# A six-layer block on one core: the two expert phases written out, with turns two tiles behind, the router in two parts and the output stored in quarters

## What is computed

```python
logits = xf @ gate_w                      # gate_w is 128 x 8
scores = softmax(logits)
top_scores, top_idx = top_k(scores, 2)
scale = zeros((T, 8)).at[arange(T)[:, None], top_idx].set(top_scores)
xs = scale.T[:, :, None] * xf[None, :, :]
h = silu(einsum('etd,edh->eth', xs, w1)) * einsum('etd,edh->eth', xs, w3)
out = einsum('eth,ehd->etd', h, w2).sum(axis=0)   # 8 experts, hidden 64
```

## Time and profile before

| | |
|---|---|
| runs, us | 2304.22, 2305.01, 2311.65 (median 2305.01) |
| profiled execution, its own time | 2300.82 us |
| its span, first to last instruction | 2299.0 us |
| mean granted TensorE clock | 0.959 of full speed |
| busy PE / DVE / ACT / POOL | 2071.4 / 1740.1 / 1378.8 / 1001.9 us |
| DMA | 144.78 MB, mean 63 GB/s |

### The profile page before, as it was taken

One profiled execution on the slowest core, in us unless ns is written; L12 is line 12 of the kernel. 1 busy time (PEld: TensorE's weight loads), 2 busy tenths in 40 slices (PEclk: granted clock), 3 DMA queues, 4 the chain that ended last, 5 costly groups with the idle time before them and its releaser, 6 DMA issues. The chain is left out here.

```text
span 2299.0 us, 41230 instructions
## 1 busy us (share of the span) xinstructions
PE 2071.4 (90%) x14740; PEld 1520.2 (66%) x14740; DVE 1740.1 (76%) x3007; ACT 1378.8 (60%) x2687; POOL 1001.9 (44%) x1475
## 2 busy tenths in 40 slices
PE   5899999987999987999999868799999999998978
PEld 4576666755777764767667645577686776775745
DVE  5766666666777758666666755599999999999953
ACT  1666666664777764666666643548558477575422
POOL 2445454524666655454555403043343443333423
PEclk7899999998999997999999989899999999999979
DMA  5555555520000005555555431000000000000000
GB/s 167 140 141 139 136 141 140 142 53 1 2 1 2 1 3 132 138 139 141 142 137 138 112 145 44 0 1 1 1 1 1 1 1 1 1 1 0 1 14 19
DMA packets 147459, 144.78 MB, mean 63 GB/s; under 512 B 14272, under 2 KB 107072, under 8 KB 146368
## 3 DMA queue, kind: packets, MB, share of 16 engines
q1 hardware_dynamic: 127680, 132.78, 21.2%
q10 hardware_dynamic: 19584, 9.44, 2.3%
HBM read 93.94 MB, written 38.80 MB: 58 GB/s over the span
## 5 line engine op out<-in xcount | busy, mean ns | idle before, releaser
L614 DVE TENSOR_REDUCE sb_f_mx<-ps_f_s 128x2 f32<-128x512 f32 x768 | 504.3, 686 | 250.3 <-PE ps_f_s L352 248.7
L538 ACT ACTIVATE sb_f_pt<-ps_f_t 128x1024 f32<-128x1024 f32 x384 | 382.0, 1024 | 62.7 <-PE ps_f_t L369 56.5
L1968 POOL TENSOR_TENSOR sb_mb_h<-sb_mb_h 128x512 f32<-128x512 f32 x128 | 165.9, 1317 | 490.7 <-DVE sb_mb_h L1828 490.7
L352 PE MATMUL ps_f_s<-sb_f_stack 96*128 96x256 bf16 x1536 | 287.9, 280 | 25.9 <-DVE sb_f_mx L614 12.8
L1823 DVE TENSOR_TENSOR_SCAN sb_mb_h<-sb_mb_da,sb_mb_h 128x1024 f32<-128x1024 f32 x128 | 291.1, 2313 | 2.1 <-ACT sb_mb_da L1687 2.1
L1536 PE MATMUL ps_mb_f<-sb_mb_fc,sb_mb_cw 128*128 128x256 f32 x1280 | 285.3, 381 | 2.0 <-ACT sb_mb_fc L1701 2.0
L1536 PEld LDWEIGHTS ps_mb_f<-sb_mb_fc,sb_mb_cw 128*128 128x128 f32 x1280 | 240.4, 190 | 37.0 <-ACT sb_mb_fc L1701 4.3
L1687 ACT ACTIVATE sb_mb_da<-sb_mb_dl,sb_mb_an 128x255 f32<-128x255 f32 x512 | 211.4, 496 | 54.9 <-DVE sb_mb_h L1823 39.4
L369 PE MATMUL ps_f_t<-sb_f_stack 128*128 128x256 bf16 x1536 | 232.6, 274 | 1.4 <-ACT sb_f_pt L538 1.4
L352 PEld LDWEIGHTS ps_f_s<-sb_f_stack 96*128 96x128 bf16 x1536 | 139.7, 99 | 113.3 <-issue 43.5
L433 PE MATMUL ps_f_a<-sb_f_pt,sb_f_v 128*32 128x256 f32 x3072 | 187.0, 384 | 2.0 <-issue 2.0
(11 more groups left out here) (256 smaller groups left out, 4154.9 us busy)
## 6 DMA issues: line engine op xcount, KB each, us to landing
f_scr<-sb_f_parts SPq DMA_DIRECT2D x96, 384.0 KB, 2.7
sb_f_stack<-f_scr SPq DMA_DIRECT2D x192, 192.0 KB, 3.1
sb_f_stack<-f_scr SPq DMA_DIRECT2D x192, 128.0 KB, 3.1
sb_f_stack<-f_scr SPq DMA_DIRECT2D x192, 64.0 KB, 3.4
sb_f_stack<-sb_f_mrow ACTq DMA_DIRECT2D x96, 96.0 KB
sb_mb_cw<-in_cw SPq DMA_DIRECT2D x1, 5120.0 KB, 19.5
sb_m_w<-in_w SPq DMA_DIRECT2D x6, 256.0 KB, 2.8
sb_prep_weT<-in_weT SPq DMA_DIRECT2D x1, 1152.0 KB, 7.3
```

Of the source, the lines that this page charges most:

```text
L352: last = nc.tensor.matmul(s_bank[j % 2][:, h, :], stack[0:ROWS, a.n % STACKS, 0, g * GROUP + pair * 2 + h, half * P:(half + 1) * P], stack ...
L538: nc.scalar.activation(pt[:, e.two, g, half, :, :], t_bank[i % 2][:, :, :], ACT.Exp).then_inc(s["pt_sb"], 1)
L614: nc.vector.tensor_reduce(mx[:, a.two, half, head:head + 2], s_bank[j % 2][:, :, :], AX.X, ALU.max)\
L1968: nc.gpsimd.tensor_tensor(hb[:, c, 0:2, :], hb[:, c, 0:2, :], hb[:, c, 2:4, :], ALU.add).then_inc(s["half_sb"], 1)
```

## The change

The two expert phases have no hardware loop any more: every engine goes over the steps 0 to 19, and in step s PE turns tile s-2, makes the up products of tile s and the down product of tile s-2; ACT copies hT of tile s-2 and takes Silu of tile s; DVE finishes tile s-3, scales tile s and, in the first expert phase, takes statistics and mean and variance of tile s-4. PE reads `k.xT` itself, and the copies to `xb` on POOL are gone. The router is in two parts: tiles 0 to 3 ahead of the steps, tiles 4 to 15 after step 1, with the logits of the parts in two PSUM banks. The second expert phase stores x in four transfers, each as soon as its four tiles are finished, and `store_phase` is gone. The diff, cut:

```diff
@@ -1102,6 +1102,10 @@
 EXPERTS, HID = 8, 64
 
 
+GATE_A = 4
+TURN_E, DONE_E = 2, 3
+
+
...
         tot = k.sb(f"{tag}_tot", [P, TT], ctx)
+        inv = k.sb(f"{tag}_inv", [P, TT], ctx)
...
-        xb = k.sb(f"{tag}_xb", [P, 2, P], ctx)
...
+        parts = (slice(0, GATE_A), slice(GATE_A, TT))
+        logits_ps = [yp[g][:, 0:TT * EXPERTS].rearrange("p (t e) -> p t e", e=EXPERTS) for g in range(2)]
+        steps = range(TT + DONE_E + 1)
+
+        def tile(step, lag):
+
+            return step - lag if 0 <= step - lag < TT else None
 
...
+            else:
+                for g in range(TT // 4):
+                    sp.wait_ge(s["x_sb"], 4 * g + 4)
+                    sp.dma_start(d["out"][:, 4 * g:4 * g + 4, :], k.x[:, 4 * g:4 * g + 4, :]).then_inc(s["stored"], 16)
+                sp.wait_ge(s["stored"], 16 * (TT // 4))
 
+            def logits(g):
+
+                for t in range(parts[g].start, parts[g].stop):
+                    pe.wait_ge(front.xT_sb, t // 4 + 1)
+                    last = nc.tensor.matmul(logits_ps[g][:, t, :], k.xT[:, t * P:(t + 1) * P], wg[:, :], start=True, stop=True)
+                last.then_inc(s["lg_ps"], 1)
+
+            def up(t):
+
+                if t >= 2:
+                    pe.wait_ge(s["u_sb"], t - 1)
+                else:
+                    pe.wait_ge(front.xT_sb, B // 2)
+                nc.tensor.matmul(a1[t % 2][:, :], k.xT[:, t * P:(t + 1) * P], w1[:, :], start=True, stop=True)
+                nc.tensor.matmul(a3[t % 2][:, :], k.xT[:, t * P:(t + 1) * P], w3[:, :], start=True, stop=True).then_inc(s["a_ps"], 1)
+
+            def turn(t):
+
+                pe.wait_ge(s["h_sb"], t + 1)
+                if t >= 2:
+                    pe.wait_ge(s["hT_sb"], t - 1)
+                for c in range(CH):
+                    last = nc.tensor.transpose(tp[t % 2][:, c, :], h[:, t % 2, c * P:(c + 1) * P], k.ident[:, :])
+                last.then_inc(s["tp_ps"], 1)
+
+            def down(t):
+
+                pe.wait_ge(s["hT_sb"], t + 1)
+                if t >= 2:
+                    pe.wait_ge(s["x_sb"], t - 1)
+                else:
+                    pe.wait_ge(s["sub_sb"], 2)
+                for c in range(CH):
+                    last = nc.tensor.matmul(yp[t % 2][:, 0:D], hT[:, t % 2, c, :], w2[:, c, :], start=c == 0, stop=c == CH - 1)
+                last.then_inc(s["y_ps"], 1)
+
             for b in range(B):
                 front.turn(pe, b)
             pe.wait_ge(s["loaded"], 16 * len(loads))
-            for t in range(TT):
-                pe.wait_ge(front.xT_sb, t // 4 + 1)
-                last = nc.tensor.matmul(yp[0][:, t * EXPERTS:(t + 1) * EXPERTS], k.xT[:, t * P:(t + 1) * P], wg[:, :],
-                                        start=True, stop=True)
-            last.then_inc(s["lg_ps"], 1)
...
-            def two(pair):
-
-                up(pair * 2, 0)
-                turn(pair * 2 - 1, 1)
-                down(pair * 2 - 2, 0)
-                up(pair * 2 + 1, 1)
-                turn(pair * 2, 0)
-                down(pair * 2 - 1, 1)
-
...
+            logits(0)
+            for step in steps:
+                f, t = tile(step, 0), tile(step, TURN_E)
+                if t is not None:
+                    turn(t)
+                if f is not None:
+                    up(f)
+                if t is not None:
+                    down(t)
+                if step == 1:
+                    logits(1)
 
         @block.gpsimd
...
-            def fetch(t, p):
-                if later(t, 1):
-                    pool.wait_ge(s["a_ps"], t - 1)
-                nc.gpsimd.tensor_copy(xb[:, p, :], k.xT[:, bass.ds(t * P, P)] if not isinstance(t, int)
-                                      else k.xT[:, t * P:(t + 1) * P]).then_inc(s["xb_sb"], 1)
...
+            for t in range(TT):
                 pool.wait_ge(s["g_sb"], t + 1)
-                if later(t, 1):
+                if t >= 2:
                     pool.wait_ge(s["tp_ps"], t - 1)
-                nc.gpsimd.tensor_tensor(h[:, p, :], u1[:, p, :], u3[:, p, :], ALU.mult).then_inc(s["h_sb"], 1)
-
-            def two(pair):
-                fetch(pair * 2, 0)
-                multiply(pair * 2 - 1, 1)
-                fetch(pair * 2 + 1, 1)
-                multiply(pair * 2, 0)
-
...
+                nc.gpsimd.tensor_tensor(h[:, t % 2, :], u1[:, t % 2, :], u3[:, t % 2, :], ALU.mult).then_inc(s["h_sb"], 1)
...
+            def exponent(g):
+
+                act.wait_ge(s["sub_sb"], g + 1)
+                nc.scalar.activation(lg[:, parts[g], :], lg[:, parts[g], :], ACT.Exp).then_inc(s["exp_sb"], 1)
+
...
+            exponent(0)
+            for step in steps:
+                f, t = tile(step, 0), tile(step, TURN_E)
+                if t is not None:
+                    act.wait_ge(s["tp_ps"], t + 1)
+                    if t >= 2:
+                        act.wait_ge(s["y_ps"], t - 1)
+                    nc.scalar.activation(hT[:, t % 2, :, :], tp[t % 2][:, :, :], ACT.Copy).then_inc(s["hT_sb"], 1)
+                if f is not None:
+                    act.wait_ge(s["u_sb"], f + 1)
+                    nc.scalar.activation(u1[:, f % 2, :], u1[:, f % 2, :], ACT.Silu).then_inc(s["g_sb"], 1)
+                if step == 1:
+                    exponent(1)
...
+            def gates(g):
+
+                n, own = parts[g].stop - parts[g].start, parts[g]
+
+                def wide(t):
+                    return t[:, own].rearrange("p (t o) -> p t o", o=1).broadcast_to([P, n, EXPERTS])
+
+                dve.wait_ge(s["lg_ps"], g + 1)
+                nc.vector.tensor_reduce(mx[:, own], logits_ps[g][:, own, :], AX.X, ALU.max).then_inc(s["mx_sb"], 1)
+                dve.wait_ge(s["mx_sb"], g + 1)
+                nc.vector.tensor_tensor(lg[:, own, :], logits_ps[g][:, own, :], wide(mx), ALU.subtract).then_inc(s["sub_sb"], 1)
+                dve.wait_ge(s["exp_sb"], g + 1)
+                nc.vector.tensor_reduce(tot[:, own], lg[:, own, :], AX.X, ALU.add).then_inc(s["tot_sb"], 1)
...
+                dve.wait_ge(s["pr_sb"], g + 1)
+                for t in range(own.start, own.stop):
+                    nc.vector.max(best[:, t, :], lg[:, t, :]).then_inc(s["best_sb"], 1)
+                dve.wait_ge(s["best_sb"], own.stop)
+                nc.vector.memset(best[:, own, 2:8], -1.0).then_inc(s["two_sb"], 1)
+                dve.wait_ge(s["two_sb"], g + 1)
+                for t in range(own.start, own.stop):
+                    nc.vector.match_replace(rest[:, t, :], best[:, t, :], lg[:, t, :], 0.0).then_inc(s["rest_sb"], 1)
+                dve.wait_ge(s["rest_sb"], own.stop)
+                nc.vector.tensor_tensor(gate[:, own, :], lg[:, own, :], rest[:, own, :], ALU.subtract).then_inc(s["gate_sb"], 1)
+
+            def scale(t):
+
+                dve.wait_ge(s["a_ps"], t + 1)
+                dve.wait_ge(s["gate_sb"], 1 if t < GATE_A else 2)
+                if t >= 2:
+                    dve.wait_ge(s["h_sb"], t - 1)
+                gt = gate[:, t, :].rearrange("p (e o) -> p e o", o=1).broadcast_to([P, EXPERTS, HID])
+                for u, a in ((u1, a1), (u3, a3)):
+                    last = nc.vector.tensor_tensor(u[:, t % 2, :].rearrange("p (e j) -> p e j", j=HID),
+                                                   a[t % 2][:, :].rearrange("p (e j) -> p e j", j=HID), gt, ALU.mult)
+                last.then_inc(s["u_sb"], 1)
+
+            def finish(t):
+
+                dve.wait_ge(s["y_ps"], t + 1)
+                nc.vector.scalar_tensor_tensor(k.x[:, t, :], yp[t % 2][:, 0:D], 0.5, k.x[:, t, :], ALU.mult, ALU.add)\
+                    .then_inc(s["x_sb"], 1)
+
+            def measure(t):
+
+                dve.wait_ge(s["x_sb"], t + 1)
+                nc.vector.bn_stats(stx[:, t, :], k.x[:, t, :]).then_inc(s["stx_sb"], 1)
+                dve.wait_ge(s["stx_sb"], t + 1)
+                nc.vector.bn_aggr(k.mv[:, t, :], stx[:, t, :])
...
-                for t in range(TT):
-                    dve.wait_ge(s["stx_sb"], t + 1)
-                    nc.vector.bn_aggr(k.mv[:, t, :], stx[:, t, :])
+            gates(0)
+            for step in steps:
+                f, o, z = tile(step, 0), tile(step, DONE_E), tile(step, DONE_E + 1)
+                if o is not None:
+                    finish(o)
+                if f is not None:
+                    scale(f)
+                if z is not None and following:
+                    measure(z)
+                if step == 1:
+                    gates(1)
...
-def store_phase(k):
-
-    nc = k.nc
-    with ExitStack() as ctx:
-        stored = k.sem("stored", ctx)
-        block = ctx.enter_context(nc.Block())
-
-        @block.sync
-        def _(sp):
-            sp.dma_start(k.d["out"], k.x[:, :, :]).then_inc(stored, 16)
-            sp.wait_ge(stored, 16)
...
         moe_phase(k, "m5")
-        store_phase(k)
```

(70 more changed lines are left out.)

46 lines of the change are left out of this document (6 added, 40 removed).

## The result

The changed kernel takes 2277.14 us (median of 4 runs, 2274.75 to 2280.54) against 2304.61 for the kernel before (median of 4). The ratio is 0.9874 with a 95% interval of [0.9856, 0.9893]: 27.5 us or 1.2% faster.

A forecast was written before the change was run, and what follows sets the result against it. PE standing at start, loop and end of the two expert phases was taken as the loss. Gains of 10.0 (second phase), 8.0 (first) and 1.9 us (store) sum to 19.9: 2305.0 - 19.9 = 2285.1 us, range 2278 to 2294.

The forecast's parts named there:

- What bounds the kernel: Both expert phases: not DMA; PE loses time in three places, start, loop and end.
- The loop: Expert loops: transposing two tiles behind fits the 3.56 us handover under 3.96 us of PE work; period 3.07 instead of 3.42.
- The slack: Loop: 0.4 us left over when the up-to-turn latency lies under neighbouring tiles' PE work.
- The router: Start of second phase: split router, clock rising at 2232 as now, logits done 2233.2, turn(2) at 2241.5.
- case D: Clock: rises early and does not drop after the pause; time 2280 us, chance 0.07.
- rival A: Clock: falls after the new 2.1 us pause before turn(2) in both phases; costs 4 us, time 2289, chance 0.13.
- the walk: First phase: logits 0.9, up(0) 1.7, up(1) at low clock 3.2, logits 4.4; turn(2) at 1380.6, 8.0 us gained.
- Queued behind on ACT: Start of the steps: PE's 2.1 us pause stands before turn(2), behind second gates, scale(2), Silu and handovers.
- Tables, POOL copies, weight loads: Expert phases: two more table switches at 1.28 us, sixteen POOL copies gone, next weights landed in time; no time effect.
- The ends: First phase: sixteen aggregates shrink to 0.95 us of last statistics; final store in four transfers gains 1.9 us (0.8 to 3.1).
- B: Loop: DVE or POOL slips, handover stays the bound at 3.42 us; 8.4 us less gain, time 2293.5, chance 0.15.
- C: Written-out steps: instruction supply stalls PE, 12 x 3.5 = 42 us, time 2327, chance 0.04.

The follow-up runs named there:

- turn_one_behind: Changed kernel with transposes only one tile behind the up products, the order of the kernel before: median 2294.5 us, period 3.33 us a tile.
- one_router: Changed kernel with its router in one part again, all sixteen logits and one selection ahead of the steps: median 2291.8 us.
- narrow_first: Changed kernel with all 32 router products ahead of the first up products on PE, DVE's selection still in two parts: 2299.1 us (1 run).
- copy_before_silu: Changed kernel with ACT copying transposed tile 1 before it takes Silu of tile 2: 2281.6 us (1 run).
- old_ends: Changed kernel with both ends as before, sixteen aggregates at the first phase's end and one 1 MB store behind the barrier: median 2286.9 us.
- selection_spread: Changed kernel with six tiles in the router's first part and the second selection on DVE cut into five pieces over steps 1 to 5: median 2274.4 us.

## Why the prediction fell short

**What bounds the kernel: right.** The sum of PE's passes, the handover that did not fit, and the router before the loop were the three places, and each edit at one of them moved it.

**The loop: right, by its size and its mechanism.** Forecast 3.07 us a tile, measured 3.05; turn_one_behind brought the wait back. The 3.42 of the loops is better read thus: with one tile between, a tile's handover on the other engines (3.56 us) and PE's turn, down and up behind it (2248.37 to 2251.65, 3.28, as the transposes take 0.66 there and not 0.44) make two periods, 6.84 us. Written out, the handover of turn_one_behind is 3.38 us and the 3.28 stay: 6.66, or 3.33 a tile. The 0.18 us between the two handovers are DVE and POOL starting later behind their operands in the loops. The slack was right too: in the changed kernel POOL is done 3.33 us after up, and turn starts at 3.77.

**The router: the step that failed.** The sum put "logits done at 2233.2 if the clock rises at 2232 as now". That is 18.1 us after the phase's start; measured were 14.7 (the 24 products end at 2220.6, start 2205.88). From there to turn(2) 8.3 us were forecast and 8.4 measured, the twelve periods took 36.6 for 36.8, the end 5.6 for 5.25. So the whole miss of 3.1 us in the second phase sits in that one term, the moment at which the clock rises: forecast 16.9 us after the start, measured 10.1. The clock did not rise "as now", because that moment hung on the run of 32 narrow products, and the change cuts it after 8 and lets the wide ones begin at 6.9 us instead of 12.1. one_router and narrow_first, which put the 32 together again, bring the rise back to 16.8 and 17.0 us. The prediction had an early rise without a fall only as case D, with 0.07. It gave back the gain of the early rise for a low clock after the pause, and that did not come: the clock stayed at full level there. The swing between two levels that the Trainium skill has at rival A ("TensorE: Matmul & The Clock Gate", "A second HAM failure mode: psum-queue depth-cycling") did not show over the 2.19 us pause of the changed kernel's second phase; in copy_before_silu the clock did fall behind the 2.16 us pause, from 23.9 to 27.4 us.

In the first phase 1.95 us were missed: turn(2) at 22.2 us, not 24.0. There the clock stayed up until 12 us, over both up products and most of the 24 router products (done at 12.7 us, not 15.7), where the walk had taken up(1) at the low level and the router products at 4.4 us. From there to turn(2) it took 9.6 us, not 8.3, since the clock was low from 12 to 19. This part is in some measure luck: in old_ends, with the same instructions up to there, the clock rose at 13 us and turn(2) came at 24.7, later than forecast.

**Queued behind on ACT: missed, without cost.** The prediction put PE's pause before turn(2). It was before down(1), since the copy of tile 1 stands behind Silu(2) on ACT. Its length, 2.1 forecast and 2.2 measured, and its cause, DVE's selection, were right (copy_before_silu, selection_spread).

**Tables, POOL copies, weight loads: right.** The loads before the exponentials took 1.28 us each; the second lies at 2220.04 to 2221.32 with its operand ready at about 2221.2, so here it is on the chain by 0.1 us, where the forecast had 1.5 us to spare. The added 1.38 us of drain that the Trainium skill counts ("ScalarE: Activation LUTs", "What ACT_TABLE_LOAD costs") doesn't show: Silu ends at 2220.02, the load runs from 2220.04, and the exponential starts at 2221.34.

**The ends: right, a little low.** Aggregates and statistics as forecast; the last quarter landed in 2.3 us, not 2.8.

**Rivals.** B did not occur (POOL's multiplies stay at 1.26 us beside DVE's scale). C did not: in the written-out steps no wait without a releaser is longer than 0.52 us, and those are weight loads beside a busy PE. The prediction's remark against C, that the other stalls of the phase behind are below 0.6 us, misread: two waits make up the 4.5 us there, so the other is 1.0. A and D were the two sides of the clock, and in the second phase it was D. The first phase was neither: an early clock and then a low one from 12 to 19 us.

**The range: a second term, and chance.** For the one profiled execution the sum was 4.5 us too high (2280.9 against 2276.40), about what case D allowed for. To get the median, it added the 4.2 us by which the runs' median lay above the profiled execution before, as if that were fixed; after the change it was 0.7. With 4.2 the result would have been 2280.6, inside the range. The same kernel measured twice more gave 2279.49 and 2279.05, inside it too. So the clock is why the forecast was some 4 us high, and that the first median fell 0.9 us out of the range is the spread of the runs, which its low end left out.

## What to carry to other kernels

When an edit moves, shortens or cuts a stretch of narrow products, don't carry over the moment at which the clock rose before; count it from the first wide products. In the second phases here it rose 2.8 to 5.5 us behind the first of them (in two kernels it was up before the router). Two edits at one latency can be worth nearly twice their separate gains: with one tile of lead, splitting the router let PE stand before the first transposes with 24 router products queued behind them. And a long block of small work on one engine can be cut into pieces that fit the spare time of a step; that gave the 4 to 5 us that beat the change.

## What was not expected of the hardware

- A busy PE did not have the full clock for it: in narrow_first PE worked without a break from the transposes on, and through all 6.83 us of products of 8 columns 0.50 was granted. In the first phase of the kernel before the clock even fell from its full level during them, at 8.5 us, while PE was busy without a break.
- The whole program's time moves by several us in parts that no edit touched: the start of the first expert phase lay between 1354.2 and 1366.5 us over 13 profiles, and the Mamba phase took 780.4 to 784.3. A single total can't settle an edit worth 5 us here; a phase inside the trace repeated to 0.1 us in three profiles of the same program.
- A 1 MB store from SBUF landed in 3.9 us in one profile and 5.5 in another.
